# Local attention layers: inverse roots taken by ScalarE through logarithm and exponential instead of a square root and VectorE's reciprocal

## What is computed

```python
def l2norm(t):
    return t / jnp.clip(jnp.linalg.norm(t, axis=-1, keepdims=True), 1e-12)
def _layer(x, wqkv, qs, ksc, wo, lg, lb, w1, b1, w2, b2):
    h = shift_token(x)
    q, k, v = jnp.split(h @ wqkv, 3, axis=-1)          # 8 heads of 64
    q = l2norm(q) * qs
    k = l2norm(k) * ksc
    q, k = rotary_xpos(q, k)
    o = local_attention(q, k, v)                        # windows of 64
    x = x + o @ wo
    h = shift_token(x)
    mu = h.mean(-1, keepdims=True)
    var = h.var(-1, keepdims=True)
    h = (h - mu) / jnp.sqrt(var + 1e-05) * lg + lb
    a, g = jnp.split(h @ w1 + b1, 2, axis=-1)
    x = x + (a * gelu(g)) @ w2 + b2
```

## Time and profile before

| | |
|---|---|
| time, median of 3 runs | 1781.65 us (1781.13 to 1785.91) |
| profiled execution, its own time | 1786.18 us |
| its span in the trace | 1784.4 us |
| local layers, from the first to the last instruction of the loop | about 1212 to 1594 us of the span |
| busy share of the span | PE 95%, DVE 83%, ACT 80%, POOL 79% |

### The profile page before, as it was taken

One profiled execution on the slowest core, in us unless ns is written; L12 is line 12 of the kernel. 1 busy time (PEld: TensorE's weight loads), 2 busy tenths in 40 slices (PEclk: granted clock), 3 DMA queues, 4 the chain that ended last, 5 costly groups with the idle time before them and its releaser, 6 DMA issues. The chain is left out here.

```text
span 1784.4 us, 54229 instructions
## 1 busy us (share of the span) xinstructions
PE 1695.4 (95%) x22798; PEld 1085.9 (61%) x22798; DVE 1473.7 (83%) x2680; ACT 1423.0 (80%) x1795; POOL 1413.1 (79%) x851
## 2 busy tenths in 40 slices
PE   6999999999999999999999999987989999988997
PEld 3566666666666666666666666684656666653554
DVE  5999989988988999899889888556988888854885
ACT  2788889898988989889898899825988888853563
POOL 6799999999999999999999999865755666625022
PEclk9999999999999999999999999999999999999988
DMA  5001010010101011010110100051211111100000
GB/s 144 25 25 30 22 30 25 25 29 25 29 23 29 25 26 28 23 31 23 28 27 24 27 21 2 7 168 25 47 38 37 37 38 38 34 21 0 1 1 24
DMA packets 76650, 56.14 MB, mean 31 GB/s; under 512 B 34764, under 2 KB 69752, under 8 KB 76408
## 3 DMA queue, kind: packets, MB, share of 16 engines
q1 hardware_dynamic: 76408, 52.69, 11.5%
HBM read 13.76 MB, written 1.05 MB: 8 GB/s over the span
## 5 line engine op out<-in xcount | busy, mean ns | idle before, releaser
L317 POOL TENSOR_TENSOR ah_probs_lo<-ah_probs,ah_probs_hi 128x1024 f16<-128x1024 f32 (+1 forms) x512 | 1059.7, 2108 | 36.1 <-ACT ah_probs L538 36.1
L613 DVE TENSOR_REDUCE ah_part_max<-ah_p_m 128x1 f32<-128x512 f32 x1024 | 667.8, 684 | 104.0 <-PE ah_p_m L381 94.5
L533 ACT ACTIVATE ah_probs_hi<-ah_p_s 128x1024 f16<-128x1024 f32 x512 | 545.6, 1066 | 117.3 <-PE ah_p_s L402 115.9
L538 ACT ACTIVATE ah_probs<-ah_p_s 128x1024 f32<-128x1024 f32 x512 | 549.1, 1072 | 0.0
L418 PE MATMUL ah_p_o<-ah_v_hi,ah_probs_hi 128*128 128x65 f16 x4096 | 470.6, 194 | 1.8
L420 PE MATMUL ah_p_o<-ah_v_lo,ah_probs_hi 128*128 128x64 f16 x4096 | 471.1, 193 | 0.0
L422 PE MATMUL ah_p_o<-ah_v_hi,ah_probs_lo 128*128 128x65 f16 x4096 | 470.9, 194 | 0.0
L420 PEld LDWEIGHTS ah_p_o<-ah_v_lo,ah_probs_hi 128*128 128x128 f16 x4096 | 378.1, 98 | 95.7
L418 PEld LDWEIGHTS ah_p_o<-ah_v_hi,ah_probs_hi 128*128 128x128 f16 x4096 | 384.2, 98 | 75.2 <-POOL ah_probs_lo L317 9.8
L381 PE MATMUL ah_p_m<-ah_k_hi_lo,ah_q_hi_twice 128*128 128x512 f16 x1024 | 388.4, 380 | 1.4 <-DVE ah_part_max L613 1.3
L401 PE MATMUL ah_p_s<-ah_q_hi_twice,ah_k_hi_lo 128*128 128x512 f16 x1024 | 388.2, 379 | 0.8 <-ACT ah_probs L538 0.3
(11 more groups left out here) (329 smaller groups left out, 3139.6 us busy)
## 6 DMA issues: line engine op xcount, KB each, us to landing
ba_v_skew<-ba_v_own SPq DMA_DIRECT2D x64, 129.0 KB, 2.3
ah_q_hi_twice<-ah_hi SPq DMA_DIRECT2D x232, 32.0 KB, 1.9
ah_k_hi_lo<-ah_hi SPq DMA_DIRECT2D x116, 32.0 KB, 1.8
ah_one_k_hi<-ah_hi SPq DMA_DIRECT2D x116, 32.0 KB, 1.9
ah_k_hi_lo<-ah_lo SPq DMA_DIRECT2D x116, 32.0 KB, 1.9
ah_max_q_lo<-ah_lo SPq DMA_DIRECT2D x116, 32.0 KB, 1.9
bw_rot<-in_rot SPq DMA_DIRECT2D x4, 512.0 KB, 10.0
ao_wqkv<-in_wqkv SPq DMA_DIRECT2D x2, 768.0 KB, 7.3
```

The costliest lines, as they stand in the source:

```text
L317: pool.tensor_tensor(pl[:, p % RW, ks, :], pb[:, p % RP, ks, :], ph[:, p % RW, ks, :], ALU.subtract).then_inc(lo_pool, 1)
L533: act.activation(ph[:, p % RW, :, :], p_s[:, p % 2, :, :], ACT.Exp, scale=HD ** -0.5)
L538: act.activation(pb[:, p % RP, :, :], p_s[:, p % 2, :, :], ACT.Exp, scale=HD ** -0.5).then_inc(exp_done, 1)
L613: dve.tensor_reduce(part[:, t, 2 * half + b:2 * half + b + 1], p_m[:, b, :], AX, ALU.max).then_inc(maxed, 1)
```

## The change

The root and the reciprocal become one pair on ScalarE: the logarithm of the clamped sums (logs), then the exponential of minus half of it straight into rnorm. VectorE's reciprocal goes. The logarithm stands ahead of the copy hTh, the exponential where the square root stood. One table set that holds both functions is named by hand: once ahead of the loop, and again behind the Gelu of each group. GpSimd's clamp waits for the logarithm instead of the root. The semaphore's renaming in the two long lists is cut here to one line.

```diff
--- before.py
+++ after.py
@@ -871,6 +871,7 @@
 FIRST_G = GROUP + 6
 LATE_G = CHUNKS - 2
 STEPS_B = TILES + 6
+LOG_AND_EXP = "natural_log_exp_and_others"
 PROB_SHIFT = 12 * float(np.log(2.0))
 RT, RV, RS, RH = 3, 4, 4, 3
 VL = HEADS_B * (DH + 1)
@@ -991,7 +992,7 @@
         sq = sc.sb("sq", [P, 2, INNER])
         ssq = sc.sb("ssq", [P, 2, 2 * HEADS_B + 1])
         ssqc = sc.sb("ssq_clamped", [P, 2 * HEADS_B + 1])
-        std = sc.sb("root", [P, 2 * HEADS_B + 1])
+        logs = sc.sb("log_sums", [P, 2 * HEADS_B + 1])
         rinv = sc.sb("rnorm", [P, 2, 2 * HEADS_B + 1])
         nshift = sc.sb("norm_shift", [P, 2])
         t12 = sc.sb("rot_parts", [P, 2, 2, INNER])
@@ -1021,13 +1022,13 @@
...
-         rq_done, rk_done, ssq_done, clamped, std_done, rooted,
+         rq_done, rk_done, ssq_done, clamped, logged, rooted,
...
@@ -1117,7 +1118,7 @@
                         if on(j - 5):
                             pool.wait_ge(var_done, j - 4)
                         if j >= 1:
-                            pool.wait_ge(std_done, j)
+                            pool.wait_ge(logged, j)
                         pool.tensor_scalar(ssqc[:, :], ssq[:, j % 2, :], 1e-24, None, ALU.max).then_inc(clamped, 1)
                     u = j - 2
                     if on(u):
@@ -1401,6 +1402,7 @@
                         act.activation(g_sb[0:n, k, :], gate_bank(m, k)[0:n, :], ACT.Gelu,
                                        bias=lw.b1[0:n, l, 1, k:k + 1]).then_inc(g_copied, 1)
 
+                act.preload_act_table_set(LOG_AND_EXP)
                 for j in range(-2, STEPS_B):
                     u = j
                     if on(u):
@@ -1450,6 +1452,11 @@
                         act.wait_ge(q_turned, u + 1)
                         act.activation(th[:, u % RT, 0, :, 0:P], p_qk[:, 0, :].rearrange("p (c t) -> p c t", t=P),
                                        ACT.Copy).then_inc(qhi_done, 1)
+                    if on(j) or on(j - 5):
+                        act.wait_ge(clamped, j + 1)
+                        if j >= 1:
+                            act.wait_ge(rooted, j)
+                        act.activation(logs[:, :], ssqc[:, :], ACT.Ln).then_inc(logged, 1)
                     u = j + 1
                     if on(u):
                         act.wait_ge(hT_turned, u + 1)
@@ -1464,10 +1471,12 @@
                         act.activation(atT[:, :, :], p_o[:, 0, :].rearrange("p (c t) -> p c t", t=P),
                                        ACT.Copy).then_inc(atT_done, 1)
                     if on(j) or on(j - 5):
-                        act.wait_ge(clamped, j + 1)
-                        if j >= 1:
-                            act.wait_ge(rooted, j)
-                        act.activation(std[:, :], ssqc[:, :], ACT.Sqrt).then_inc(std_done, 1)
+                        act.wait_ge(logged, j + 1)
+                        if on(j - 2):
+                            act.wait_ge(roped, j - 1)
+                        if on(j - 7):
+                            act.wait_ge(h2n_done, j - 6)
+                        act.activation(rinv[:, j % 2, :], logs[:, :], ACT.Exp, scale=-0.5).then_inc(rooted, 1)
                     copy_gate(j, 1)
                     copy_gate(j, 2)
                     m, r = geglu_of(j)
@@ -1478,6 +1487,8 @@
                         act.activation(g_sb[:, 0:HC - 1, :], g_sb[:, 0:HC - 1, :], ACT.Gelu)
                         act.activation(g_sb[0:LASTN, HC - 1, :], g_sb[0:LASTN, HC - 1, :],
                                        ACT.Gelu).then_inc(gelu_done, 1)
+                    if r == 0 and (on(j - 1) or on(j - 4)):
+                        act.preload_act_table_set(LOG_AND_EXP)
 
             @block.vector
             def _(dve):
@@ -1590,13 +1601,6 @@
                         dve.tensor_reduce(negm[:, u % 2, :].rearrange("p (c b) -> p b c", b=2),
                                           p_s[:, :, :].rearrange("p b (c k) -> p b c k", k=P), AX, ALU.max,
                                           negate=True).then_inc(max_done, 1)
-                    if on(j) or on(j - 5):
-                        dve.wait_ge(std_done, j + 1)
-                        if on(j - 2):
-                            dve.wait_ge(roped, j - 1)
-                        if on(j - 7):
-                            dve.wait_ge(h2n_done, j - 6)
-                        dve.reciprocal(rinv[:, j % 2, :], std[:, :]).then_inc(rooted, 1)
                     u = j - 3
                     if on(u):
                         t = u % NT
```

More of the change, by code:

```diff
@@ L1023, in local_layers @@
         (consts, cleared, hT_turned, hTh_done, hTl_done, q_ready, k_ready, squared,
-         rq_done, rk_done, ssq_done, clamped, std_done, rooted, nshift_done, t3_done, roped, k_turned, q_turned, khi_done, kxh_done, qhi_done,
+         rq_done, rk_done, ssq_done, clamped, logged, rooted, nshift_done, t3_done, roped, k_turned, q_turned, khi_done, kxh_done, qhi_done,
          klo_done, kxl_done, qlo_done, v_ready, vh_done, vl_done, s_ready, max_done, st_ready, exp_done,
@@ L1029, in local_layers @@
              "consts", "cleared", "hT_turned", "hTh_done", "hTl_done", "q_ready", "k_ready",
-             "squared", "rq_done", "rk_done", "ssq_done", "clamped", "std_done", "rooted", "nshift_done", "t3_done", "roped", "k_turned",
+             "squared", "rq_done", "rk_done", "ssq_done", "clamped", "logged", "rooted", "nshift_done", "t3_done", "roped", "k_turned",
              "q_turned", "khi_done", "kxh_done", "qhi_done", "klo_done", "kxl_done", "qlo_done", "v_ready",
```

## The result

The changed kernel takes 1796.2 us (median, 1788.85 to 1798.95) where the kernel before takes 1781.75 (1780.67 to 1785.91) beside it: 1.0061 times as long, 95% interval 1.0048 to 1.0074. By the ratio that is 10.9 us (the two medians lie 14.4 apart; the runs of one kernel scatter over 5 and 10 us). It is slower, though ScalarE has 57 fewer table loads. The profiled execution is 1798.95 us long, its span 1797.2.

A forecast was written before the change was run, and what follows sets the result against it. Three engines were nearly full, with a closed loop of ScalarE and TensorE pacing ordinary steps. Terms -2.1 - 0.9 + 3.9 + 1.0 - 0.5 = +1.4 us gave a median of 1783.0 us, range 1775.5 to 1788.5.

The forecast's parts named there:

- Ordinary steps: Steps 3 to 9: the exponential starts 0.30 us earlier, then waits for TensorE's scores; 9.59 to 9.29 each, -2.1 us.
- rival A: ScalarE's body, not TensorE's scores, sets the pace in all steps: sum -6.0 us, 1775.7; chance 0.14.
- rival B: Every table load is exposed, so removing them saves 73 us: 1708.5; chance 0.02.
- Gate steps: Six steps: squares 1.41 us later behind the load named by hand, 0.76 gained elsewhere; 0.65 longer each, +3.9 us.
- Rival C: Gate steps: load named exposed whole, third gate projection no earlier; 6 x 1.41, sum +6.0 us, 1787.7; chance 0.11.
- D: A table load has a hidden drain, a second 1.28 us behind each of six: +7.7 on top, 1790.7; chance 0.03.
- E: The set named by hand doesn't last; logarithm and exponential get own loads each step: +36 us, about 1819; chance 0.03.
- Reciprocal: VectorE's 0.18 us slot goes through in the second down step of a group only: five steps, -0.9 us.
- Start: Step 0: hTh stands behind the logarithm, 1.0 us later, and tile 1's projection hangs on it: +1.0 us.
- End: Step 33: without the root, x_mid starts when the projection ends: -0.5 us (0 to -0.8).
- Value steps: VectorE runs on from the squares; its chain holds neither load nor reciprocal: no change, 0 us.

The follow-up runs named there:

- e1: Changed kernel with the table load named by hand moved from behind the Gelu to behind the next step's squares: 1779.54 us, 0.9978 of the kernel before.
- e5: Changed kernel with two extra, unused projections of v on TensorE in each value step: 1786.63 us, 1.0002 of the kernel before.
- e8: Changed kernel with four extra, unused projections of v on TensorE in each value step: 1786.35 us, 1.0008 of the kernel before.
- e3: Kernel before, with the exponentials' table load named by hand behind the Gelu, ahead of the squares, in six gate steps: 1796.65 us, 1.0069 of the kernel before.
- e4: Changed kernel with the load moved behind the squares and the logarithm moved behind the copy hTh: 1776.84 us, 0.9956 of the kernel before.

## Why the prediction was wrong

The forecast was 1783.0 us, 1775.5 to 1788.5, with a chance of 0.17 for slower; 1796.2 was measured. The sum priced the direct effects nearly rightly and had no term for TensorE's clock.

- *Ordinary steps.* Right in mechanism: 9.29 forecast, 9.28 to 9.30 measured from step 7 on. The exponential waits for TensorE, 0.06 behind its scores, so rival A fell too. The forecast took seven steps at 9.59; before, steps 3 to 5 took 9.1 and only four took 9.59. Steps 4 to 9 gave 1.64 where 1.8 was forecast, step 3 lost in the start's clock. That nearly all of ScalarE's 73 us would bring only the 0.30 by which it had been late is the part to learn from; rival B fell.
- *Gate steps.* Right in mechanism, and in part by luck in the sum: +3.9 forecast, +3.89. The squares moved by the forecast 1.41; the projection came 0.66 earlier where 0.76 was taken. Step 10 got only 0.20 longer, the other five 0.69 to 0.88. Rival C's whole 1.41 did not come; D's drain neither, as the squares start 0.02 behind the load; E's extra loads neither (15).
- *Reciprocal.* Wrong in size and place: -0.9 was forecast for the second down steps; all ten down steps together gave -0.27. Three second down steps gave 0.12 each instead of 0.18, and two got longer behind VectorE's waits without a releaser. The two value steps that these waits left got 0.3 shorter each, which the forecast had at nothing. Nothing of it shows in the runs' times.
- *Start.* The direct part was right (+1.0 forecast, 0.93 in e1). The forecast had no term for the clock, and the stretch came out at +3.06; how much of that belongs to the change is open, as the clock of this stage differs from kernel to kernel without order.
- *End.* -0.51 where step 31 ran at the full clock (e5, e8), as forecast. In the profile after it was +0.21 and in the second +1.32: step 31 is a value step too, has the same idle time in front of its transposes, and ran at 0.85 and 0.70.
- *Value steps: the step that failed.* They were priced at nothing because "its chain holds neither load nor reciprocal". That sums durations of the trace of before as if they were fixed. The rows had been read at the full granted clock (ordinary steps; no row of a value step was taken, but they too ran at 1.00), and the forecast itself said that the squares would come 1.41 later and that VectorE would be idle nearly 5 us on them. It stopped there and didn't ask what TensorE does meanwhile: it waits for VectorE too, 2.54 instead of 1.11 us. Behind that its clock fell, for +2.4 us over the five steps in one profile and +7.0 in another, and with step 31 more. Rival C had asked what a later square costs directly; no rival asked what an idle TensorE costs afterwards.

In sum, with the value steps held at the full clock by filler the layers are 3.8 us longer than before, where the forecast had 1.4. The difference is the start (+3.0 for 0.7); value steps (-0.6 for 0) and down steps (-0.3 for -0.9) cancel. What goes beyond that is shown to hang on the idle time: e3 brings it about in the kernel before by the load's place alone, e1 and e4 take it away by the same place, e5 and e8 take most and all of it away without touching anything but TensorE's idle time. The Trainium skill, page "TensorE: Matmul & The Clock Gate", section "What's actually happening", says that the granted clock depends on how busy TensorE has been recently; the table of value steps agrees. It also says there that the same kernel comes out differently from run to run; the two profiles of the changed kernel, with one value step kept at 1.00 and four at 0.74 in the second, agree.

## What to carry to other kernels

When an edit makes an engine later, follow the lateness on to TensorE and compare its idle time before and after, also where the step ahead of it has slack: in this case the price was paid behind the wait, in products at the lower clock. A table load that must be somewhere goes behind the last instruction that others wait for and into a wait of ScalarE's own; here moving them from in front of the squares to behind them turned +0.6% into -0.2%. And fewer loads were worth only what the first instruction behind each was late by.

## What the hardware showed that was not expected

- In a value step the clock falls and is back at 1.00 in the next step; a fall costs 0 to 2.0 us of a value step (11.25 to 13.25), by whether the slow products stand on the path. The mean clock of a whole execution shows little of it: 0.979 against 0.990.
- In value steps with step 31, an idle time of 2.5 us was followed by the lower clock in 29 of 30 cases, one of 1.1 to 1.25 in 3 of 30. The length alone doesn't decide.
- VectorE had two waits of 0.2 to 0.3 us without a releaser in a profile at the full clock; they stood in value steps 11 and 15 with the reciprocal and at the end of steps 20 and 24 without it.
- Useless products in place of a wait gave back 9 us (1795.59 to 1786.63).
